# Decoder layer on one core: state, key and value products of the attention moved between slots, heads unpermuted, first iteration reordered

## What is computed

```
x = layernorm(x + linear_attention(x))     # 16 heads of 16, no softmax: q (k^T v), two k/v sets multiplied, norm, Wo
x = layernorm(x + cross_attention(x, ctx)) # 16 heads of 64, 64 context rows per batch, softmax, Wout
x = layernorm(x + experts(x))              # 8 experts 256 -> 1024 -> 256, relu, first 1024 tokens of each are taken
```

## Time and profile before

| | |
|---|---|
| runs | 1253.24, 1251.56, 1249.86 us, median 1251.56 |
| the profiled execution | 1252.67 us, span 1251.0 us |
| PE busy | 1204.5 us (96%) |
| DVE busy | 864.4 us (69%) |
| ACT, POOL busy | 554.0 us (44%), 584.7 us (47%) |
| mean granted TensorE clock | 0.989 of 2.4 GHz |

### The profile page before, as it was taken

One profiled execution on the slowest core, in us unless ns is written; L12 is line 12 of the kernel. 1 busy time (PEld: TensorE's weight loads), 2 busy tenths in 40 slices (PEclk: granted clock), 3 DMA queues, 4 the chain that ended last, 5 costly groups with the idle time before them and its releaser, 6 DMA issues.

```text
span 1251.0 us, 27297 instructions
## 1 busy us (share of the span) xinstructions
PE 1204.5 (96%) x10512; PEld 1053.0 (84%) x10512; DVE 864.4 (69%) x1694; ACT 554.0 (44%) x1097; POOL 584.7 (47%) x968
## 2 busy tenths in 40 slices
PE   7986999999999999999999999989999999999998
PEld 6875888888888888888888888877799899899888
DVE  4653888889889889888888898988533323332435
ACT  2122555555555565555555555555513412421420
POOL 1323666566656656666665666655322112202201
PEclk9987999999999999999999999999999999999999
DMA  9931011111120110111111110220222022021001
GB/s 235 232 92 35 10 51 53 35 52 46 33 61 20 59 58 21 60 44 36 52 52 35 53 50 28 84 88 26 94 68 68 1 68 68 1 68 68 1 1 35
DMA packets 92774, 70.09 MB, mean 56 GB/s; under 512 B 45667, under 2 KB 86372, under 8 KB 92645
## 3 DMA queue, kind: packets, MB, share of 16 engines
q1 hardware_dynamic: 90612, 67.67, 18.5%
q10 hardware_dynamic: 2032, 0.66, 0.2%
HBM read 42.09 MB, written 26.22 MB: 55 GB/s over the span
## 4 chain that ended last, share of the span: by engine, by line
PE 76%; issue 6%; DVE 6%; POOL 4%; ACT 1%; POOLq 0%; DVEq 0%
PE sim L137 7%; PE sim L138 6%; PE sim L139 6%; PE ob L137 6%; PE ob L138 5%; PE ob L139 5%; PE pt L500 4%; PE pw L392 3%; PE pw L137 2%; PE pt L139 2%; PE pt L138 2%; PE pt L137 2%; PE pw L455 2%; PE pw L138 2%; PE pw L139 2%
## 5 line engine op out<-in xcount | busy, mean ns | idle before, releaser
L1625 POOL TENSOR_TENSOR w_lo<-w_raw,w_hi 128x2048 fp32r<-128x2048 f32 x16 | 73.7, 4609 | 221.0 <-ACT w_hi L1565 167.8
L137 PE MATMUL ob<-b_hi,pT_hi 128*128 128x256 f32 x512 | 151.4, 296 | 0.0
L138 PE MATMUL ob<-b_lo,pT_hi 128*128 128x256 f32 x512 | 144.2, 282 | 0.0
L139 PE MATMUL ob<-b_hi,pT_lo 128*128 128x256 f32 x512 | 144.0, 281 | 0.0
L967 POOL TENSOR_TENSOR prob<-prob,rz 128x512 f32<-128x512 f32 x128 | 130.9, 1044 | 12.5 <-DVE rz L814 12.5
L724 ACT ACTIVATE prob<-prob 128x512 f32<-128x512 f32 x128 | 81.1, 633 | 99.7 <-DVE prob L868 99.6
L137 PEld LDWEIGHTS ob<-b_hi,pT_hi 128*128 128x128 f32 x512 | 97.3, 190 | 8.3 <-issue 5.4
L730 ACT ACTIVATE pT_hi<-pt 128x512 fp32r<-128x512 f32 x128 | 76.1, 595 | 53.5 <-PE pt L500 52.3
L138 PEld LDWEIGHTS ob<-b_lo,pT_hi 128*128 128x128 f32 x512 | 97.5, 191 | 1.9
L139 PEld LDWEIGHTS ob<-b_hi,pT_lo 128*128 128x128 f32 x512 | 96.8, 189 | 0.0
L882 POOL TENSOR_SCALAR ve<-mv 128x1 f32<-128x1 f32 x128 | 27.9, 218 | 142.7 <-DVE mv L772 142.5
(11 more groups left out here) (244 smaller groups left out, 3724.9 us busy)
## 6 DMA issues: line engine op xcount, KB each, us to landing
xraw<-in_x SPq DMA_DIRECT2D x16, 512.0 KB, 4.0
kv_scratch<-stage SPq DMA_DIRECT2D x32, 256.0 KB, 3.9
x_scratch<-x SPq DMA_DIRECT2D x64, 128.0 KB, 1.7
out_x<-o_sb SPq DMA_DIRECT2D x64, 128.0 KB, 1.7
w_raw<-in_L_ffn_experts_inter SPq DMA_DIRECT2D x8, 1024.0 KB, 5.1
w_raw<-in_L_ffn_experts_out SPq DMA_DIRECT2D x8, 1024.0 KB, 7.6
kraw<-kv_scratch SPq DMA_DIRECT2D x16, 256.0 KB, 2.9
vraw<-kv_scratch SPq DMA_DIRECT2D x16, 256.0 KB, 2.8
```

The lines of the kernel that those rows point to most:

```text
L137: pe.matmul(out, lh, rh, start=first, stop=False)
L138: pe.matmul(out, lh, rl, start=False, stop=False)
L139: return pe.matmul(out, ll, rh, start=False, stop=last)
```

## The change

The tables move preps between places. G goes from behind pT to ahead of the score halves (new place 0), GT and R beside tr in slot 0, B0 to the end of slot 0, B2 and ST from between the score halves to behind them, A1 to the end of slot 2. So plain fp32 products lie beside the plain transposes, in 9 blocks a batch in place of 14. On DVE B0, B2, A1 and ST get later places too. In iteration -1 the keys A come in slots 0 and 1, and SB, SW and Q in slot 0 of iteration 0. POOL does g_lo at the end of slot 0 and r_prod at the end of slot 1. The heads are kept in their own order: rows of Wkv and Wq and columns of Wout are loaded as they lie, and the high and low parts of A and B are written to other columns instead.

```diff
     ORDER = {
-        "G": ((0, 3), (0, 6), (0, 8)), "GT": ((0, 5), (0, 7), (0, 8)),
...
+        "G": ((0, 0), (0, 1), (0, 8)), "GT": ((0, 4), (0, 7), (0, 8)), "R": ((0, 4), (0, 7), (0, 8)),
...
-        "ST": ((3, 1), (3, 1), (3, 3)),
...
+        "ST": ((3, 2), (3, 1), (3, 5)),
...
     FIRST_ORDER = {
...
+    SECOND_ORDER = {"G": ((0, 3), (0, 6), (0, 8))}
...
-        rest = [n for n in NAMES if n != "R"]
+        keys = [n for n in NAMES if n[0] == "A"]
+        rest = [n for n in NAMES if n[0] != "A"]
         i = rest.index("T1")
-        return rest[:i] + ["R"] + rest[i:]
+        return rest[:i] + keys + rest[i:]
...
         if h == 0:
             need(pe, "tr_taken", n + 2)
             if slot == 0:
-                prep_done(pe, it - 1, last_of("A0", "A1"))
+                prep_done(pe, it - 1, last_of("A0", "A1", "A2", "A3"))
                 need(pe, "mask_in_a", 16 * (it + 1))
-        elif slot == 0:
-            prep_done(pe, it - 1, last_of("A2", "A3"))
...
         if has_prev:
             pe_pT(pe, n - 1, (slot - 1) % 2, 0)
+        prep(0)
         if has_sim:
             pe_sim(pe, it, slot, 0)
...
         if name[0] == "A":
-            return pw[:, :], *folded_keys(batch_of(name, it), i % 2, i // 2)
-        return (pw[:, :].rearrange("p (r c) -> p r c", r=2), b_hi[:, 2 * i:2 * i + 2, :],
-                b_lo[:, 2 * i:2 * i + 2, :])
+            hi, lo = (a[batch_of(name, it) % 2][i % 2].rearrange("p (q g x) -> p g q x", g=2, x=P)[:, i // 2]
+                      for a in (a_hi, a_lo))
+            return pw[:, :].rearrange("p (q x) -> p q x", x=P), hi, lo
+        chunks = slice(i // 2 * 4 + i % 2, i // 2 * 4 + 4, 2)
+        return pw[:, :].rearrange("p (r c) -> p r c", r=2), b_hi[:, chunks, :], b_lo[:, chunks, :]
...
-        if slot == SPLIT_SLOT and within(it + 2) and it != -2:
-            pool_split(pool, it)
-        if slot == STATE_SLOT and has_state(it):
-            pool_sums(pool, it)
...
         if tile_exists(n + 5) and it != -1:
             pool_xb(pool, n + 5, it + 1 if slot < 3 else it + 2, (slot + 1) % 4, par(1 if slot < 3 else 2))
+        if slot == SPLIT_SLOT and has_state(it):
+            pool_split(pool, it)
+        if slot == SUMS_SLOT and has_state(it):
+            pool_sums(pool, it)
...
         def load_wkv(g):
             q = slice(4 * g, 4 * g + 4)
-            for half in range(2):
-                sp.dma_start(wkv_raw[half * NKV:(half + 1) * NKV, q, :],
-                             (wkv_keys, wkv_values)[g // 2][half, g % 2]).then_inc(wkv_loaded[g], 16)
+            sp.dma_start(wkv_raw[:, q, :], wkv_chunks[:, q, :]).then_inc(wkv_loaded[g], 16)
```

More of the change, by code:

```diff
@@ L228, in place_in @@
     def place_in(eng, name, j):
-        return (FIRST_ORDER.get(name, ORDER[name]) if j == -1 else ORDER[name])[ENGINES.index(eng)]
+        return {-1: FIRST_ORDER, 0: SECOND_ORDER}.get(j, ORDER).get(name, ORDER[name])[ENGINES.index(eng)]
     def batch_of(name, it):
@@ L293, in at @@
         out = []
-        for n in NAMES:
-            for j in (it, it - 1):
+        for j in (it - 1, it):
+            for n in NAMES:
                 sl, pl = place_in(eng, n, j)
@@ L634, in act_norm @@
         act.activation(dst, src, ACT.Identity, bias=nmr[:, q, ln:ln + 1], scale=rstd[:, q, ln:ln + 1]).then_inc(s[done], 1)
-    SPLIT_SLOT = 1
+    SPLIT_SLOT = 0
+    SUMS_SLOT = 1
     STATE_SLOT = 2
@@ L1201, in load_ctx @@
             sp.dma_start(ctx_raw[:, q, :], ctx_tiles[:, q, :]).then_inc(ctx_loaded[h], 16)
-        wkv_keys = t["L0_xattn_Wkv"][0:PAIRS * P, :].rearrange("(g a i d) c -> g a d i c", g=2, a=2, d=NKV)
-        wkv_values = t["L0_xattn_Wkv"][PAIRS * P:2 * PAIRS * P, :].rearrange("(a g i d) c -> g a d i c", g=2, a=2, d=NKV)
-        wq_halves = t["L0_xattn_Wq"].rearrange("(g i d) c -> g d i c", g=2, d=NKV)
+        wkv_chunks = t["L0_xattn_Wkv"].rearrange("(i p) c -> p i c", p=P)
         def load_wkv(g):
             q = slice(4 * g, 4 * g + 4)
-            for half in range(2):
-                sp.dma_start(wkv_raw[half * NKV:(half + 1) * NKV, q, :],
-                             (wkv_keys, wkv_values)[g // 2][half, g % 2]).then_inc(wkv_loaded[g], 16)
+            sp.dma_start(wkv_raw[:, q, :], wkv_chunks[:, q, :]).then_inc(wkv_loaded[g], 16)
         load_ctx(0)
@@ L1240, in _ @@
                 if n == 6:
-                    for half in range(2):
-                        sp.dma_start(wqx[half * NKV:(half + 1) * NKV, :, 1:C + 1], wq_halves[half]).then_inc(loaded["wqx"], 16)
+                    sp.dma_start(wqx[:, :, 1:C + 1], t["L0_xattn_Wq"].rearrange("(r p) c -> p r c", p=P)).then_inc(loaded["wqx"], 16)
                 if n == 8:
@@ L1248, in _ @@
                 if n == 14:
-                    for m in range(MC):
-                        for quarter in range(4):
-                            a, half = quarter // 2, quarter % 2
-                            cols = slice(quarter * C, (quarter + 1) * C)
-                            sp.dma_start(wout_raw[:, m, a * W:(a + 1) * W].rearrange("p (i g d) -> p g i d", g=2, d=NKV)[:, half],
-                                         t["L0_xattn_Wout"][m * P:(m + 1) * P, cols].rearrange("p (i d) -> p i d", d=NKV)
-                                         ).then_inc(loaded["wout"], 16)
+                    sp.dma_start(wout_raw[:, :, :], t["L0_xattn_Wout"].rearrange("(m p) d -> p m d", p=P)).then_inc(loaded["wout"], 16)
             if u == PREPS[4]:
@@ L1315, in _ @@
             if i == 2:
-                pool.wait_ge(loaded["wqx"], 32)
+                pool.wait_ge(loaded["wqx"], 16)
                 pool.tensor_tensor(wqx[:, :, 1:C], wqx[:, :, 1:C], wqx[:, :, C:C + 1].broadcast_to([P, PAIRS, C - 1]), ALU.subtract)
@@ L1344, in _ @@
             elif kind == "wkvT":
-                pe.wait_ge(wkv_loaded[it[2]], 32)
+                pe.wait_ge(wkv_loaded[it[2]], 16)
                 for i in range(4):
@@ L1353, in _ @@
             elif kind == "wox":
-                pe.wait_ge(loaded["wout"], 64 * MC)
+                pe.wait_ge(loaded["wout"], 16)
                 for r in range(2):
```

## The result

The changed kernel took **1267.27 us** (median, 1267.2 to 1268.13) against 1252.06 for the kernel before in the same comparison: a ratio of 1.0124, 95% interval 1.0108 to 1.014. Its profiled execution has a span of 1265.5 us, 14.5 more than before. The forecast was 1266.

A forecast was written before the change was run, and what follows sets the result against it. It took slot 3 to be bound by the chain DVE, POOL, ACT, DVE ahead of Q0, not PE. 1252.67 + 18.0 - 3.0 - 0.5 = 1267.2 us profiled, less 1.1 for the median: 1266, range 1256 to 1274.

The forecast's parts named there:

- ST behind both score halves: Slot 3: ST's low part ends 1.33 us later, delaying sprod, nmr, x2, zw_hi, zw_lo and Q0 by 1.33 a batch.
- the signs: Profile after: Q0 1.8 to 2.1 us behind the products, x2 waiting 2.4 or more, POOL 3.5 or more, period near 49.8.
- Low parts of A1 and A3: Slot 3: standing ahead of DVE's pT_lo they may add 0.1 to 0.2 us; the batch sum took 0.05.
- The upper bound of 1.7: Upper bound in us on the net cost a batch, forecast at 1.28 with lower bound 0.8.
- Fewer blocks: Five plain fp32 blocks merged a batch: about 0.35 us saved on PE, of which 0.1 counts, bounds 0 and 0.6.
- drain rule: Tiling mode changes drain TensorE, so the four tiled blocks save nothing and only GT's 0.17 us is left.
- PE isn't the bound in slot 3: Q0 begins as DVE's first part of zw_lo ends, so the chain DVE, POOL, ACT, DVE bounds slot 3.
- G ahead of the scores: Slot 0: scores come 2.64 us later, but z set the probabilities' time; counted 0, bounds 0 and +0.5 a batch.
- The rival that G brings a second wait: Slot 0's probabilities come 0.5 us late for slot 1 in 14 batches: 7 us more, 1273 to 1280; chance 0.12.
- Setup: Unpermuted weight loads need fewer transfers; only first waits count, the second issued one DMA sooner: -0.5 us, bounds 0 and -1.
- Iteration -1: Keys A fill earlier gaps and scores fill idle time around SB, the low clock staying: -3.0 us, bounds 0 and -6.
- Last two batches: No state products; waits for probabilities take what the moved B blocks save: 0, bounds -1 and +1.5 us.

The follow-up runs named there:

- experiment 11: Changed kernel with ScalarE's SB and SW between transposes' copy and norms, plus A1 and A3 put back to slot 2: 1241.92 us, ratio 0.9925.
- experiments 7: Changed kernel with ST, G, GT, R and Q1's low part put back: 1246.62 us, ratio 0.9959.
- experiment 8: Changed kernel with ST and Q1's low part put back, G left ahead of the scores: 1251.76 us, ratio 1.0001.
- experiment 9: Kernel before with the heads unpermuted alone (fewer weight loads, split copies), its order as it was: 1248.59 us, ratio 0.9979.
- experiments 2: Kernel before with ST alone moved as in the change, behind the second score half: 1269.57 us, ratio 1.0138.
- experiment 5: Kernel before with ScalarE's SB and SW between the transposes' copy and the norms, nothing else: 1252.49 us, ratio 0.9999.
- experiment 10: Changed kernel with ScalarE's SB and SW between copy and norms, plus iteration -1's SB, SW, Q0, Q1 ahead of the scores again: 1245.29 us.
- 12: Changed kernel with ScalarE's SB and SW between copy and norms, plus Q1's low part late in batch 14 only: 1245.12 us, ratio 0.9952.

## Why the prediction was right, and where it only seemed so

- **ST behind both score halves: +1.33 a batch. Right**, in size and way. Undone it gives back 1.31, done alone it costs 1.29, and cut at ScalarE's link it costs nothing. Of the signs, x2 waited 3.06 us for nmr (at least 2.4 was said) and POOL 4.20 for ST (at least 3.5); Q0's wait was 1.40, not 1.8 to 2.1. The saving ahead of it, which I added, is mostly in slot 0, where it shortens the batch and not this wait. Two small readings were off: the first part of zw_lo ended at 553.93 in the kernel before, not near 554.1 (the parts are unequal, and Q0 at 553.98 still follows it); and sbdT was to bring "no wait of its own", but SB waits for it by 0.17 us, which Q0's wait covers here and experiment 11 lays open.
- **Low parts of A1 and A3: +0.05. Too small**: 0.19 (experiment 11), the top of the "0.1 to 0.2" that the text gave and then took as 0.05. Slot 3 with ST put back, 13.33 in place of 13.13, has the same 0.2. Both edits move A1's and A3's products on PE too. (The upper bound of 1.7 has no term of its own: 1.33 and 0.2 are 1.53.)
- **Fewer blocks: 0.1 of 0.35. Too small.** Slots 0 to 2 are together 0.25 us shorter (35.48 before, 35.23 after). With 0.19 and 1.31 the sum is +1.25, the measured 1.27 within what the means can tell. Two errors of 0.15 cancelled, which is luck. R's four products (0.44 us) went from slot 1 to slot 0; with them set aside, slot 0 (G, GT, R, B0) is 0.26 shorter and slot 1 (B2) is not. What the Trainium skill's drain rule (TensorEngine Tiling (Array Packing), Key Properties) leaves, 0.17, and my 0.35 lie on either side of 0.25, so no run here decides between them; G's and Q1's moves are in the same slots. That B2 saved nothing is on the rule's side.
- **"PE isn't the bound in slot 3": right by 0.2 us only**, and the chain named was one of two that ended together. In the kernel before, DVE's own queue released zw_lo; cutting ScalarE's link there changed nothing. That both stood without slack, and PE had only 0.2 us, made the forecast come true, not that the one named was the bound.
- **G ahead of the scores: 0. The value right, the reason incomplete.** The prediction didn't price Q1's low part ahead of pT's, which alone would cost 1.0 us a batch. It was read as a small shift of place; G's 2.64 us on PE cover it. The rival that G brings a second wait (0.12) fell: apart from Q1 it costs 0.3, as experiments 7 and 8 show, and with it nothing.
- **Setup: -0.5. Wrong size**: -2.9 by the medians. The step that failed is the price of the first waits: one of them was said to end one DMA sooner. Two waits (0.86 and 1.00 us) went, and the products behind them no longer start at the slow distance of 0.43 us (experiment 9). I counted transfers and not packets, of which the changed kernel has 4035 fewer; whether these are the cause is not shown.
- **Iteration -1: -3.0. Right sign, too large.** From the setup's G to the first pT of slot 1 it is 50.9, 51.3, 49.2 and 49.4 us in four profiles with the old order, and 47.1 to 50.0 (mean 48.4, nine profiles) with the new: about -1.8, with ranges that overlap. The two profiles compared above happen to lie 3.1 apart. SB waited 4.99 us, as said (4 to 6). On the clock, windows of 2 us have 0.50 from 108 to 112 and 0.93 from 112 on, after the wait of 4.99 us. The low level came again, as forecast. Behind SB it stayed for 4.2 us, against 5.8 behind the 7.28 us of before. But the filled gap isn't shown to have shortened it: in the other three profiles of the old order it stayed for 2.7 us behind the same 7.28, and in the nine of the new for 4.2 to 5.6 behind 3.2 to 5.0. The Trainium skill (TensorE: Matmul & The Clock Gate, Part 1) has the low level come after idle time, and the trace agrees. What a gap filled altogether would do was not tested: it was filled only in part.
- **Last two batches: 0. Wrong**: +4.5 in the profiled execution. Slot 0 of batch 14 is 1.04 longer, by Q1's low part, which has no G to cover it there (with it put back, in experiment 8, the slot is 10.01 as before). Slot 3 is 0.44 longer, by the A parts (10.56 with them put back in experiment 11, 10.54 before). Slot 2 of batch 14 and slot 0 of batch 15 are 1.56 and 1.49 longer by the clock. The first of these isn't the change's doing: experiments 2, 5 and 9, in the kernel before's order, have 12.57 or 12.58 there too. The second may be: it is 9.9 in nine of ten profiles in the changed order, and 8.3 in one; in the order of before it is 8.4 in three of four. The wait ahead of it, 3.00 in the changed kernel and 2.57 before, doesn't settle it: the 8.3 stands behind 3.00 us (experiment 10), and two of the 9.9 behind 2.54 and 2.58 (experiments 11 and 2). And what slot 0 is spared comes later: slots 0 to 2 of batch 15 together are 31.1 to 31.3 us in six profiles, three of either order, and 32.7 to 32.8 in eight.

So the 1266 rests on one large term that was right, and on errors of the small ones that nearly cancel: setup 2.4 us too little gain, iteration -1 1.2 too much, the end some 1.5 to 4.5 too little loss. That it came within 1.3 us of 1267.27 is luck.

## What to carry to other kernels

An instruction that is moved for one engine's sake is moved in four queues: follow each of them to the next engine, and ask of each move what it waits for and what stands behind it, since the price is paid by the latter. Where a chain costs, look for the link where an instruction merely stands behind an unrelated wait; there the repair (24 us from two lines) may be worth more than undoing the move. Two moves in one slot can each be bad and together be good, so test them in all four combinations before either is called harmless.

## What the hardware showed that was not expected

- A fall of TensorE's clock is not settled by the wait ahead of it. In slot 2 of batch 14, behind a wait of 2.20 to 2.26 us and with the same work, seven of the fourteen profiles have 10.99 to 11.03 us and a granted clock of 1.00, and seven 12.56 to 12.59 and 0.86, nothing between: a fall costs 1.56 us, or none comes. Of differences of 1 or 2 us between two kernels a part may be just this, as in 11 and 12.
- Loads of weights in a permuted order and in more transfers let the setup end at 77.9 to 80.8 us, in plain order and fewer transfers at 75.9 to 76.3.
- A wait of 0.2 us doesn't show in the waits. It does in the distance between the starts of two products: 0.30 where 0.12 is usual (Q0 in experiment 5), 1.60 over twelve of them where 1.42 is usual (SB in experiment 11).
